# Query and key columns by dimension then head, replicas by three transfers a set

## The chip, the cores and the metric

One core of one Trainium2 chip. The time is the device time of one execution in microseconds (us); a kernel's time is the median of its runs.

## The reference

A cross-attention layer on normalised `x` (8 batches of 512 rows, 256 wide), then a feed-forward layer that is the sum of a dense path (self-attention with 16 heads of 16, and a SiLU network) and a mixture of experts. The change touches the queries and keys of the dense path:

```python
q = (x @ wq).reshape(b, s, H, hd)            # H = 16 heads, hd = 16, s = 512
k = (x @ wk).reshape(b, s, H, hd)
scores = jnp.einsum('bqhd,bkhd->bhqk', q, k) / np.sqrt(hd).astype(np.float32)
scores = jnp.where(causal, scores, jnp.finfo(scores.dtype).min)
attn = jax.nn.softmax(scores, axis=-1)
```

## The kernel before

A program walks the eight batches. Each engine has one instruction queue, taken in order, and all queues follow one list written out by hand, `STEPS`: while batch `b` has its cross-attention, projections and row maxima, batch `c = b - 1` has its attention scores, its SiLU network and its end. Waits are on counting semaphores (`need(engine, batch, name, count)`), `done` counts one up. The first batch has no `c`; in its walk 16 steps `kv` (keys and values of the cross-attention for all batches, stored by ACT's queue to `kt_d` and `vt_d`) take the place of the other work.

Queries and keys are float32 and are multiplied in bf16 as sums of three parts (`part1`, `part2`, `part3`). A score is the sum of six products of parts: q1k1, q1k2, q2k1, q2k2, q1k3, q3k1. To have the six in one product of contraction 96, q and k are replicated: `q_rep` and `k_rep` have 96 rows, one for each of 6 products and each of 16 dimensions, with 16 heads x 512 positions of bf16 = 16,384 bytes in each row. A row is put together through HBM:

- step `qk a` (a = 0, 1 queries, 2, 3 keys; 128 columns each): PE multiplies, ACT makes part 1 (L1178) and part 2 (L1181, L1184), DVE the rest (L1460), POOL part 3 (L720). Each part is a tile of 128 partitions (8 heads x 16 dimensions, head first) x 512 positions.
- SP's queue stores each of the 12 parts to `parts_d` (L524), 128 rows of 1,024 bytes. `parts_d` is (part, q or k, dimension, head, half, position).
- when the six query stores have landed (`q_out`) ACT's queue issues six transfers to `q_rep` (L1202), in the step `route 0`, ahead of the exponential of the router (L1204). When the six key stores have landed (`k_out`) SP's queue issues six to `k_rep` (L531). Each brings 16 rows of 16,384 bytes, one for each dimension. Behind them in SP's queue stand the loads for the next batch (`load_kv`, L451; `load_x`, L444).
- PE goes on with steps `fu` and `fd` (L1033, L1043) of batch `c`, and ranks the router's choice. Then the first step `max` waits for `slot`, `rep_q` and `rep_k` (L942 to L944) before its products (L955, L956), whose maxima DVE takes (L1519). All the 32 `max` steps of a batch and the rest of `fu` and `fd` stand behind it in PE's queue.

The weights `wq` and `wk` are loaded once, with their columns as in the input (head, then dimension). `yb` is a buffer of 1,024 floats a partition that is not used before the end of the first batch.

Of the kernel before, what the change touches and what calls it, by code (L numbers as in the profile page):

```python
# [17 lines left out]
P = 128  # L18
B, S, D = 8, 512, 256
T = S // P  # L20
KD = D // P
CH, CHD, CK = 16, 64, 64
PAIRS = CH // 2
H, HD = 16, 16
NREP = 6
KREP = NREP * HD
# [13 lines left out]
PBUF = 4  # L40
EW_EARLY = 6

Q_PART = (0, 0, 1, 1, 0, 2)
K_PART = (0, 1, 0, 1, 2, 0)

UNITS = 10
CHUNKS = 3
# [6 lines left out]
    sc_ps=4, sc_add=4, sc_sub=4, sc_exp=4, sc_rec=4, sc_nrm=4,  # L54
    pT_ps=8, pT_sb=8, pv_ps=4, xb=1, x1=4, mv2=4, rstd2=4, xn2=4, xT2=2, xn2T=2,
    qk_ps=4, part1=4, rest1=4, part2=4, part3=4, v_ps=4, v_sb=4, lg=4,
    q_out=96, k_out=96, rep_q=96, rep_k=96, z=1,
    gmax=1, gexp=1, mask=1, rank_ps=1, slot=1, xk=1, scat=128, dve_step=42, pool_a=4, pool_n=1,
    a_ps=32, a_max=32, m_part=2, mT_ps=2, mT_sb=2, m_row0=48, m_row1=48,
    b_ps=G * UNITS, b_exp=G * UNITS, b_cut=G * UNITS, va_ps=G * CHUNKS, av_sb=4, avT_ps=4, o_rec=4, o_nrm=4,  # L60
# [139 lines left out]
def xattn_ffn(nc, A, out):  # L200
    per = PER
    counted = {}
    with ExitStack() as ctx:
        def sb(name, shape, dt=F32):
            return ctx.enter_context(nc.sbuf_tensor(name, shape, dt))

        def sem(name):
            return ctx.enter_context(nc.semaphore(name))
# [2 lines left out]

        sems = {n: sem(n) for n in per}
        kv_out = [sem(f"p0_kv_out{i}") for i in range(4)]
        p0 = {n: sem("p0_" + n) for n in ("w_first", "bias_ps", "w_early", "w_mid", "w_late", "w_up", "kv0_ps", "norms", "split_hi", "split", "ident", "const", "iota", "tr_ps", "tr_sb", "kv_ps", "kv_sb", "bk")}

        moe = {n: sem("moe_" + n) for n in ("table_step", "table", "ids_off", "ids", "ew_in", "zero", "gate", "xT_ps", "xT", "up_ps", "th", "u", "g", "gT_ps", "gT", "dn_ps", "eo")}
        xs_in = [sem(f"xs_in{i}") for i in range(4)]
# [6 lines left out]
        wq = sb("wq", [P, KD, D])  # L224
        wk = sb("wk", [P, KD, D])
# [6 lines left out]
        bk = sb("bk", [P, PAIRS])  # L232
# [5 lines left out]
        ident = sb("ident", [P, P])  # L238
# [25 lines left out]
        def part(a, n):  # L264
# [14 lines left out]
        q_rep = part(20480, 4096).bitcast(BF16).rearrange("p (h n) -> p h n", h=H)  # L279
        k_rep = part(24576, 4096).bitcast(BF16).rearrange("p (h n) -> p h n", h=H)  # L280
# [30 lines left out]
        xk_id = part(11264, T * XW).rearrange("p (t w) -> p t w", t=T)  # L311
        yb = sb("yb", [P, T, D])
        hb = sb("hb", [P, T, D])
        xnT = sb("xnT", [P, KD, S])
        xn2T = sb("xn2T", [P, KD, S])
        o_tok = sb("o_tok", [P, T, D])
# [2 lines left out]
        parts = [xnT[:, :, :].rearrange("p k n -> p (k n)").bitcast(BF16).rearrange("p (a n) -> p a n", a=4),  # L319
                 part(13312, 1024).bitcast(BF16).rearrange("p (a n) -> p a n", a=4),  # L320
                 part(14336, 1024).bitcast(BF16).rearrange("p (a n) -> p a n", a=4)]
# [63 lines left out]
        parts_d = internal("parts_d", (3, 2, HD, H // KD, KD, S), BF16)  # L385
# [4 lines left out]
        def done(ins, name, n=1):  # L390

            counted[name] = counted.get(name, 0) + n
            return ins.then_inc(sems[name], n)

        def need(eng, b, name, k):

            eng.wait_ge(sems[name], b * per[name] + k + AHEAD.get(name, 0))
# [42 lines left out]
        def _(sp):  # L440
# [28 lines left out]
            load_x(0)  # L469

            def load_late_weights():
                for dst, src in ((wq, "L0_ffn_wq"), (wk, "L0_ffn_wk")):
                    sp.dma_start(dst[:, :, :], A[src].rearrange("(k p) n -> p k n", p=P)).then_inc(p0["w_late"], 16)
                sp.dma_start(wv[:, :, 0:D], A["L0_ffn_wv"].rearrange("(k p) n -> p k n", p=P)).then_inc(p0["w_late"], 16)
                sp.dma_start(wv[:, :, D:D + E], A["L0_ffn_router_w"].rearrange("(k p) n -> p k n", p=P)).then_inc(p0["w_late"], 16)
                for dst, src in ((wo, "L0_ffn_wo"), (w2, "L0_ffn_w2")):
                    sp.dma_start(dst[:, :, :], A[src].rearrange("(k p) n -> p k n", p=P)).then_inc(p0["w_late"], 16)
                for dst, src in ((aw_bc, "L0_ffn_attn_norm_w"), (fw_bc, "L0_ffn_ff_norm_w"), (mw_bc, "L0_ffn_moe_norm_w")):
                    sp.dma_start(dst[:, :], A[src].partition_broadcast(P)).then_inc(p0["w_late"], 16)
# [35 lines left out]
            def batch(b, c, end=False, only=None):  # L515
                if c is not None:
                    send_shifts(c, 1)
                if b is not None:
                    if c is None:
                        load_late_weights()  # L520
                    for a in range(4):
                        for i, name in enumerate(("part1", "part2", "part3")):
                            need(sp, b, name, a + 1)
                            done(sp.dma_start(parts_d[i, a // 2, :, :, a % 2, :].rearrange("d h n -> h d n"), parts[i][:, a, :]), ("q_out", "k_out")[a // 2], 16)  # L524
                    if c is not None:
                        need(sp, c, "b_ps", per["b_ps"])
                        sp.sem_inc(freed, 1)
                    need(sp, b, "k_out", per["k_out"])
                    for j in range(NREP):
                        src = parts_d[K_PART[j], 1, :, :, :, :].rearrange("d h a n -> d (h a n)")  # L530
                        done(sp.dma_start(k_rep[j:KREP:NREP, :, :].rearrange("d h n -> d (h n)"), src), "rep_k", 16)  # L531
                    if not (isinstance(b, int) and b == B - 1):
                        if c is not None:
                            load_kv(b + 1)
                        load_x(b + 1)
                    send_shifts(b, 0)
                    if c is None:
                        for i in range(4):
                            sp.wait_ge(kv_out[i], 16 * 2 * PAIRS // 4)
                        sp.sem_inc(freed, 1)  # L540
                        load_kv(b + 1)
                    if c is None:
                        need(sp, b, "q_out", per["q_out"])
                        need(sp, b, "pv_ps", per["pv_ps"])
                        need(sp, b, "scat", per["scat"])
                        sp.sem_inc(freed, 1)
                        for dst, src in zip(w13_in, ("L0_ffn_w1", "L0_ffn_w3")):
                            sp.dma_start(dst, A[src].rearrange("(k p) n -> p k n", p=P)).then_inc(p0["w_up"], 16)
                    if b == B - 1:
                        need(sp, b, "pv_ps", per["pv_ps"])  # L550
                        need(sp, b, "q_out", per["q_out"])
                        sp.sem_inc(freed, 1)
                        need(sp, b, "scat", per["scat"])
                        load_experts(range(EW_EARLY))
                if b is None:
                    experts_first()
                elif c is not None:
                    need(sp, c, "y", 1)
                    done(sp.dma_start(at_batch(y_d, c), hb[:, :, :]), "y_out", 16)
# [231 lines left out]
        def _(pe):  # L791
# [31 lines left out]
            def batch(b, c, end=False, only=None):  # L823
# [10 lines left out]
                for step in only or walked(b, c, end):  # L834
                    kind = step[0]
                    if kind == "kv":
                        i = step[1]
# [4 lines left out]
                        w = (wk_c, wv_c)[i % 2]  # L842
# [5 lines left out]
                    elif kind == "m":  # L848

                        i = step[1]  # L850
                        k, half = i // 2, i % 2
# [8 lines left out]
                    elif kind == "bqk":  # L860

                        i = step[1]
# [6 lines left out]
                    elif kind == "vw":  # L869

                        i = step[1]
# [7 lines left out]
                    elif kind == "cs":  # L879
                        t, half = step[1:]  # L880
# [10 lines left out]
                    elif kind == "ct":  # L891
                        t, half = step[1:]
# [9 lines left out]
                    elif kind == "cv":  # L902
                        t, half = step[1:]
# [8 lines left out]
                    elif kind == "qk":  # L912

                        a = step[1]
                        if a == 0:
                            if c is None:
                                pe.wait_ge(p0["w_late"], 16 * 9)
                            need(pe, b, "xn2T", 2)
                        w = (wq, wk)[a // 2]
                        for k in range(KD):  # L920
# [2 lines left out]
                    elif kind == "v":  # L923

                        t = step[1]
# [11 lines left out]
                    elif kind == "max":  # L937

                        hp, t = step[1:]
# [11 lines left out]
                        n = (t + 1) * P  # L951
# [161 lines left out]
        def _(act):  # L1113
# [9 lines left out]
            def batch(b, c, end=False, only=None):  # L1123
# [6 lines left out]
                for step in only or walked(b, c, end):  # L1130
# [63 lines left out]
                            need(act, c, "va_ps", per["va_ps"])  # L1194
                        done(fn(v_heads[:, t, :, 0:HD], bank(t, D).rearrange("p (h d) -> p h d", h=H), ACT.Copy), "v_sb")
                    elif kind == "route" and step[1] == 0:
                        if c is not None:
                            need(act, c, "b_ps", per["b_ps"])
                        need(act, b, "q_out", per["q_out"])
                        for j in range(NREP):  # L1200
                            src = parts_d[Q_PART[j], 0, :, :, :, :].rearrange("d h a n -> d (h a n)")
                            done(act.dma_start(q_rep[j:KREP:NREP, :, :].rearrange("d h n -> d (h n)"), src), "rep_q", 16)  # L1202
                        need(act, b, "gmax", 1)
                        done(fn(g_b, g_a, ACT.Exp), "gexp")  # L1204
                    elif kind == "sc":
# [91 lines left out]
        def _(dve):  # L1297
# [72 lines left out]
            def batch(b, c, end=False, only=None):  # L1370
# [21 lines left out]
                for step in only or walked(b, c, end):  # L1392
# [56 lines left out]
                    elif kind == "qk":  # L1449
                        a = step[1]  # L1450
                        if a == 0 and c is None:

                            dve.wait_ge(p0["w_late"], 16 * 9)
                            for w in (aw_bc, fw_bc, mw_bc):
                                v.tensor_scalar(w[:, :], w[:, :], float(D) ** 0.5, None, ALU.mult).then_inc(p0["norms"], 1)
                            dve.wait_ge(p0["norms"], 3)
# [201 lines left out]
```

## Time and profile before

| | us |
|---|---|
| median of 3 runs (lowest, highest) | 1511.2 (1509.92, 1518.62) |
| profiled execution, its own time | 1514.02 |
| its span on the core | 1512.2 |
| PE busy | 1376.5 (91%) |
| DVE, POOL, ACT busy | 811.6, 601.4, 575.4 |
| mean granted clock of TensorE | 0.962 of full speed |

A busy PE is not a PE at its peak. "SPq" and "ACTq" are the queues of SP and ACT that issue DMAs; the time of such a row is that of the issue, not of the transfer. The DMA share in a window is the mean busy share of the core's 16 DMA engines; it can read above 1 where packets wait on each other. "L955" is line 955 of the kernel.

### The profile page before, as it was taken

How to read it: one execution, taken by the hardware profiler on the slowest of the kernel's cores; microseconds unless marked ns; L12 is line 12 of the kernel's file. 1: busy time of each engine (PE TensorE's matmuls, PEld its weight loads, DVE VectorE, ACT ScalarE, POOL GpSimd, SP SyncE). 2: the span in 40 equal slices, each digit the busy share in tenths (PEclk: the TensorE clock that was granted, in tenths of full speed). 3: DMA queues.
4: the chain of work that ended last, by engine and by line, in shares of the span. 5: the costliest groups of instructions: out<-in, count | busy, mean ns of one | idle time of the engine just before them, and what ended most of it. 6: DMA issues, size and time to landing. Idle time of an engine off the chain costs nothing.

```text
span 1512.2 us, 22383 instructions
## 1 busy us (share of the span) xinstructions
PE 1376.5 (91%) x7229; PEld 891.4 (59%) x7230; DVE 811.6 (54%) x1652; ACT 575.4 (38%) x1214; POOL 601.4 (40%) x1051
## 2 busy tenths in 40 slices
PE   6886898999899989998999899989998789999995
PEld 6543556656665666566656665666566246666673
DVE  2625655754485358436753675366546623333348
ACT  2231553055306521641255036404540444344346
POOL 4312343253325332633254235423532435555544
PEclk8998899999999999999999999999999799999997
DMA  6054205200600060006001500240031424332245
GB/s 209 1 145 138 67 1 130 53 16 1 157 26 16 1 164 19 16 10 170 18 1 39 144 16 1 78 104 16 1 105 50 152 86 129 127 100 87 86 177 197
DMA packets 77529, 115.39 MB, mean 76 GB/s; under 512 B 24072, under 2 KB 65440, under 8 KB 74880
## 3 DMA queue, kind: packets, MB, share of 16 engines
q1 hardware_dynamic: 67120, 79.68, 18.7%
q10 hardware_dynamic: 3840, 16.78, 3.9%
q0 software_dynamic: 6480, 17.77, 3.3%
q8 instruction: 52, 0.85, 0.2%
q14 instruction: 37, 0.30, 0.1%
HBM read 70.22 MB, written 43.59 MB: 75 GB/s over the span
## 4 chain that ended last, share of the span: by engine, by line
PE 66%; DVE 9%; DMA 7%; POOL 5%; ACT 5%; issue 3%; SPq 3%; ACTq 0%; POOLq 0%; DVEq 0%
PE ps L1069 8%; PE ps L1033 8%; PE ps L907 7%; PE ps L888 6%; DVE nm L1519 5%; PE ps L993 5%; PE ps L955 4%; PE ps L1086 4%; PE ps L980 4%; DMA room<-parts_d 3%; PE ps L1043 3%; DMA parts_d<-room 3%; PE ps L921 2%; PE ps L1013 2%; SPq L531 2%
## 5 line engine op out<-in xcount | busy, mean ns | idle before, releaser
L1519 DVE TENSOR_REDUCE nm<-ps 128x2 f32<-128x256 f32 (+3 forms) x256 | 202.4, 819 | 103.3 <-PE ps L956 100.9
L1211 ACT ACTIVATE room<-ps 128x512 f32<-128x512 f32 x320 | 179.7, 598 | 157.0 <-PE ps L980 156.8
L1033 PE MATMUL ps<-hT,w 128*128 128x512 f32 x768 | 212.7, 421 | 0.0
L692 POOL TENSOR_SCALAR_AFFINE_SELECT room<-room 128x256 f32<-128x256 f32 (+1 forms) x320 | 121.5, 391 | 138.3 <-ACT room L1211 133.6
L955 PE MATMUL ps<-room 96*128 96x128 bf16 (+3 forms) x512 | 129.6, 315 | 44.2 <-DMA room<-parts_d 26.5
L1033 PEld LDWEIGHTS ps<-hT,w 128*128 128x128 f32 x768 | 144.7, 196 | 33.1 <-DVE hT L1547 2.0
L1235 ACT ACTIVATE room<-ps 128x512 f32<-128x512 f32 x64 | 37.2, 593 | 294.2 <-PE ps L1033 294.2
L1043 PE MATMUL ps<-w,room 128*128 128x256 f32 x512 | 137.6, 399 | 7.5 <-DVE room L1568 7.5
L1069 PE MATMUL ps<-room 128*128 x284 | 135.4, 599 | 2.4 <-ACT room L1263 2.4
L907 PE MATMUL ps<-room 128*128 128x256 f32 x512 | 123.1, 384 | 2.7 <-ACT room L1172 1.8
L888 PE MATMUL ps<-room,xnT 128*128 128x512 f32 x256 | 122.0, 601 | 0.0
L980 PE MATMUL ps<-room 99*128 99x384 bf16 (+3 forms) x512 | 111.7, 308 | 7.9 <-ACT room L1211 6.0
L955 PEld LDWEIGHTS ps<-room 96*128 96x128 bf16 x512 | 51.6, 102 | 107.7 <-issue 46.9
L907 PEld LDWEIGHTS ps<-room 128*128 128x128 f32 x512 | 93.8, 190 | 22.7 <-issue 6.7
L956 PE MATMUL ps<-mask_qk,ident_b 128*128 128x128 bf16 x512 | 106.1, 228 | 0.0
L1043 PEld LDWEIGHTS ps<-w,room 128*128 128x128 f32 x512 | 91.7, 195 | 24.1 <-DVE room L1568 11.6
L1611 DVE COPY room<-ps 128x256 f32<-128x256 f32 x71 | 30.1, 424 | 125.9 <-PE ps L1077 125.9
L993 PE MATMUL ps<-room,v_aug 128*32 128x512 f32 (+3 forms) x1024 | 91.0, 451 | 6.1 <-POOL room L692 5.1
L1423 DVE TENSOR_TENSOR room<-ps,room 128x1024 f32<-128x1024 f32 x32 | 39.1, 1223 | 106.4 <-PE ps L888 106.4
L980 PEld LDWEIGHTS ps<-room 99*128 99x128 bf16 x512 | 42.8, 98 | 88.7 <-issue 43.7
L641 POOL TENSOR_TENSOR spare_p<-neg_half 128x1 f32<-128x1 f32 x95 | 18.4, 193 | 179.3 <-DVE room L1512 114.7
L781 POOL DMA_INDIRECT pair_d<-room,ids_u x71 | 71.8, 1012 | 33.6 <-issue 29.9
(234 smaller groups left out, 2372.3 us busy)
## 6 DMA issues: line engine op xcount, KB each, us to landing
room<-parts_d SPq DMA_DIRECT2D x48, 256.0 KB, 5.3
room<-parts_d ACTq DMA_DIRECT2D x48, 256.0 KB, 5.7
room<-xs_d SPq DMA_DIRECT2D x71, 129.0 KB, 2.1
parts_d<-room SPq DMA_DIRECT2D x64, 128.0 KB
room<-pair_d SPq DMA_DIRECT2D x8, 1024.0 KB, 8.3
room<-in_L_ffn_ew SPq DMA_DIRECT2D x24, 256.0 KB, 5.5
xin<-in_x SPq DMA_DIRECT2D x8, 512.0 KB, 8.1
parts_d<-xnT SPq DMA_DIRECT2D x32, 128.0 KB
```

Source lines behind the costliest of these rows:

```text
L692: done(g.affine_select(out=w, in_=w, compare_op=ALU.is_ge, fill=0.0, base=0, pattern=[[0, 2]] * (blocks - 1) + [[1, P]], channel_multiplie ...
L888: last = mm(bank(half), xnT[:, k, t * P:(t + 1) * P], m_sb[:, k, half * 512:(half + 1) * 512], start=(k == 0), stop=(k == KD - 1))
L907: last = mm(bank(3, D), pT[:, t % 2, a * P:(a + 1) * P], vw[:, a, :], start=(a == 0), stop=(a == PAIRS - 1))
L955: mm(bank(o, n), q_rep[0:KREP, rep_at(h), t * P:n], k_rep[0:KREP, rep_at(h), 0:n], start=True, stop=False)
L956: last = mm(bank(o, P, t * P), ident_b[:, :], mask_qk[:, :], start=False, stop=True)
L980: last = mm(ps[:, o:o + S - kb * P], k_rep[0:KREP + MROWS, h, kb * P:(kb + 1) * P], q_rep[0:KREP + MROWS, h, kb * P:S], start=True, stop=T ...
L993: last = mm(ps[32 * j:32 * j + 32, 4 * 512 + kb * P:5 * 512], v_aug[:, v_at(kb, 4 * grp + j):v_at(kb, 4 * grp + j) + 32], prob[:, at:at + ...
L1033: last = mm(bank(up_banks(b, m)[i]), w[:, x, k, m * P:(m + 1) * P], hT[:, y, k, :], start=((x, y, k) == terms[0]), stop=((x, y, k) == term ...
L1043: last = mm(bank((6, 7)[half], D, t % 2 * D), gT[:, m % 2, t * P:(t + 1) * P], w2[:, m, :], start=(m == 0 and t % 2 == 0), stop=(m == FB - ...
L1069: last = mm(bank(2 + i % 2), xsT[:, i % 2, k * P:(k + 1) * P], ew[:, bass.ds(at + k * 2 * D, 2 * D)], start=(k == 0), stop=(k == KD - 1))
L1211: done(fn(prob[:, u * 512:(u + 1) * 512], bank(6 + n % 2), ACT.Exp), "b_exp")
L1519: done(v.tensor_reduce(nm[:, t, 2 * hp:2 * hp + 2], pair_ps, AX.X, ALU.max, negate=True), "a_max")
```

## The change

The columns of `wq` and `wk` are brought into the order dimension, then head: they are loaded into `w_heads` (a view of `yb`) and DVE copies them over in the new order, once, ahead of the first `qk` step, which waits for it (`w_turned`). So the partitions of a part are 16 dimensions x 8 heads, and its store to `parts_d` is written as one run over 128 rows where it was 8 heads of 16 rows; the bytes of a row stay 1,024.

The 96 rows of `q_rep` and `k_rep` are ordered by product, then dimension, where it was dimension, then product. Each is filled by three transfers in place of six, of 3, 2 and 1 times 16 rows of 16,384 bytes: for q part 1 three times, part 2 twice, part 3 once (the source has a leading dimension of step 0); for k parts 1 to 3, 1 and 2, 1 (the source's leading dimension is the part). The six products are the same. The three for q go from ACT's queue to SP's, after the stores and ahead of k's.

```diff
-Q_PART = (0, 0, 1, 1, 0, 2)
-K_PART = (0, 1, 0, 1, 2, 0)
+REPLICAS = ((0, 3), (3, 2), (5, 1))
...
+        w_heads = yb[:, :, :].rearrange("p t d -> p (t d)").rearrange("p (i k n) -> p i k n", i=2, k=KD)
...
             def load_late_weights():
-                for dst, src in ((wq, "L0_ffn_wq"), (wk, "L0_ffn_wk")):
-                    sp.dma_start(dst[:, :, :], A[src].rearrange("(k p) n -> p k n", p=P)).then_inc(p0["w_late"], 16)
+                for dst, src in ((w_heads[:, 0, :, :], "L0_ffn_wq"), (w_heads[:, 1, :, :], "L0_ffn_wk")):
+                    sp.dma_start(dst, A[src].rearrange("(k p) n -> p k n", p=P)).then_inc(p0["w_late"], 16)
...
                             need(sp, b, name, a + 1)
-                            done(sp.dma_start(parts_d[i, a // 2, :, :, a % 2, :].rearrange("d h n -> h d n"), parts[i][:, a, :]), ("q_out", "k_out")[a // 2], 16)
+                            done(sp.dma_start(parts_d[i, a // 2, :, :, a % 2, :].rearrange("d h n -> (d h) n"), parts[i][:, a, :]), ("q_out", "k_out")[a // 2], 16)
...
+                    need(sp, b, "q_out", per["q_out"])
+                    for i, (j, n) in enumerate(REPLICAS):
+                        done(sp.dma_start(q_rep[j * HD:(j + n) * HD, :, :].rearrange("p h n -> p (h n)"), parts_d[i, 0, :, :, :, :].rearrange("d h a n -> d (h a n)").unsqueeze(0).to_broadcast([n, HD, H * S])), "rep_q", 16)
                     need(sp, b, "k_out", per["k_out"])
-                    for j in range(NREP):
-                        src = parts_d[K_PART[j], 1, :, :, :, :].rearrange("d h a n -> d (h a n)")
-                        done(sp.dma_start(k_rep[j:KREP:NREP, :, :].rearrange("d h n -> d (h n)"), src), "rep_k", 16)
+                    for i, (j, n) in enumerate(REPLICAS):
+                        done(sp.dma_start(k_rep[j * HD:(j + n) * HD, :, :].rearrange("p h n -> p (h n)"), parts_d[0:n, 1, :, :, :, :].rearrange("i d h a n -> i d (h a n)")), "rep_k", 16)
...
                                 pe.wait_ge(p0["w_late"], 16 * 9)
+                                pe.wait_ge(p0["w_turned"], 2)
...
                     elif kind == "route" and step[1] == 0:
-                        if c is not None:
-                            need(act, c, "b_ps", per["b_ps"])
-                        need(act, b, "q_out", per["q_out"])
-                        for j in range(NREP):
-                            src = parts_d[Q_PART[j], 0, :, :, :, :].rearrange("d h a n -> d (h a n)")
-                            done(act.dma_start(q_rep[j:KREP:NREP, :, :].rearrange("d h n -> d (h n)"), src), "rep_q", 16)
                         need(act, b, "gmax", 1)
...
                             dve.wait_ge(p0["w_late"], 16 * 9)
+                            for i, w in enumerate((wq, wk)):
+                                v.tensor_copy(w[:, :, :].rearrange("p k (a d h) -> p (k a) d h", a=KD, d=HD),
+                                              w_heads[:, i, :, :].rearrange("p k (a h d) -> p (k a) d h", a=KD, d=HD)).then_inc(p0["w_turned"], 1)
```

## Rows read from the trace of the kernel before

**Rows 1.** The page: span, and the chain that ended last by engine and line.
```profile
span 1512.2 us, 22383 instructions
...
PE ps L1069 8%; PE ps L1033 8%; PE ps L907 7%; PE ps L888 6%; DVE nm L1519 5%; PE ps L993 5%; PE ps L955 4%; PE ps L1086 4%; PE ps L980 4%; DMA room<-parts_d 3%; PE ps L1043 3%; DMA parts_d<-room 3%; PE ps L921 2%; PE ps L1013 2%; SPq L531 2%
```

**Rows 2.** Waits of the whole run, PE's: total, times, longest (us).
```profile
PE ps L955 <- DMA room<-parts_d: 26.5, 7, 4.3
```

**Rows 3.** The chain of waits, 388 to 416 us: start, us, what.
```profile
393.43 6.76 DMA parts_d<-room
...
403.36 0.59 SPq L531
...
403.99 7.03 DMA room<-parts_d
411.02 0.25 issue
411.27 0.27 PE ps L955
```

**Rows 4.** Timeline, 376 to 416 us: start, us, engine, line, instruction.
```profile
382.84 0.60 SPq L524 DMA_DIRECT2D parts_d<-xnT  x1
...
390.41 2.28 POOL L720 TENSOR_TENSOR room<-xin,room 128x512 bf16<-128x512 f32 x2
...
392.82 1.18 SPq L524 DMA_DIRECT2D parts_d<-room  x2
...
393.25 3.73 ACTq L1202 DMA_DIRECT2D room<-parts_d  x6
...
397.02 0.23 ACT L1204 ACTIVATE small<-small 128x32 f32<-128x32 f32 x1 [3.45 <-issue]
...
407.71 0.17 DVE L1512 COPY room<-ids_all 128x4 uint32<-128x4 uint32 x1
```

**Rows 5.** DMA from 382 to 391 us: busy tenths in 40 slices, packets.
```profile
DMA  0000000003445300000444522445554555545555
...
DMA packets 862, 0.83 MB, mean 93 GB/s; under 512 B 48, under 2 KB 862, under 8 KB 862
```

**Rows 6.** DMA from 388 to 394 us, 40 slices: busy tenths, GB/s.
```profile
DMA  4545544555454555555455555542000053435564
GB/s 171 205 171 178 171 177 177 191 178 198 177 205 171 171 171 164 191 184 157 157 198 184 191 184 198 184 171 96 27 0 0 0 102 55 75 130 205 178 191 157
```

**Rows 7.** Windows: us, busy time by engine, granted clock, DMA share of 16 engines, GB/s.
```profile
156.00:158.00 2.00, 0.88 (x5) 0.39 (x4) 2.00 (x5) 0.00 (x0) 0.00 (x0) 0.50 1.03 414
391.50:392.00 0.50, 0.50 (x4) 0.43 (x3) 0.50 (x1) 0.43 (x1) 0.50 (x2) 1.00 0.54 191
394.50:395.00 0.50, 0.50 (x3) 0.39 (x3) 0.50 (x1) 0.00 (x0) 0.50 (x1) 1.00 1.35 449
396.00:400.00 4.00, 3.44 (x16) 2.52 (x15) 2.05 (x7) 1.21 (x3) 0.00 (x0) 1.00 1.06 273
408.00:411.00 3.00, 0.00 (x0) 0.00 (x0) 0.00 (x0) 0.00 (x0) 0.15 (x1) 0.75 1.10 119
411.00:416.00 5.00, 4.73 (x17) 3.55 (x18) 1.79 (x4) 0.00 (x0) 1.08 (x1) 0.50 0.80 171
```

**Rows 8.** Timeline of the first batch, 76 to 126 us.
```profile
79.48 0.28 DVE L1455 TENSOR_SCALAR aw_bc<-aw_bc 128x256 f32<-128x256 f32 x1
...
81.05 5.37 PE L921 MATMUL ps<-xn2T,wq 128*128 128x512 f32 x8 [0.78 <-ACT xn2T L1128]
...
93.72 1.36 SPq L524 DMA_DIRECT2D parts_d<-room  x2
...
122.82 0.22 PE L955 MATMUL ps<-room 96*128 96x128 bf16 x1
```

**Rows 9.** Timeline: the first product for the maxima of the eighth batch.
```profile
1140.04 0.27 PE L955 MATMUL ps<-room 96*128 96x128 bf16 x1 [3.37 <-DMA room<-parts_d]
```

More of the change, by code:

```diff
@@ L56 @@
     qk_ps=4, part1=4, rest1=4, part2=4, part3=4, v_ps=4, v_sb=4, lg=4,
-    q_out=96, k_out=96, rep_q=96, rep_k=96, z=1,
+    q_out=96, k_out=96, rep_q=48, rep_k=48, z=1,
     gmax=1, gexp=1, mask=1, rank_ps=1, slot=1, xk=1, scat=128, dve_step=42, pool_a=4, pool_n=1,
@@ L213, in xattn_ffn @@
         kv_out = [sem(f"p0_kv_out{i}") for i in range(4)]
-        p0 = {n: sem("p0_" + n) for n in ("w_first", "bias_ps", "w_early", "w_mid", "w_late", "w_up", "kv0_ps", "norms", "split_hi", "split", "ident", "const", "iota", "tr_ps", "tr_sb", "kv_ps", "kv_sb", "bk")}
+        p0 = {n: sem("p0_" + n) for n in ("w_first", "bias_ps", "w_early", "w_mid", "w_late", "w_turned", "w_up", "kv0_ps", "norms", "split_hi", "split", "ident", "const", "iota", "tr_ps", "tr_sb", "kv_ps", "kv_sb", "bk")}
         moe = {n: sem("moe_" + n) for n in ("table_step", "table", "ids_off", "ids", "ew_in", "zero", "gate", "xT_ps", "xT", "up_ps", "th", "u", "g", "gT_ps", "gT", "dn_ps", "eo")}
```

## The prediction

> **What bounds the kernel now.** I read first the page [rows 1]: PE carries most of the chain that ended last, but two DMA entries stand in it with 3% each, `parts_d<-room` and `room<-parts_d`, and the queue's L531 with 2%. The transfers that the change touches are on the path. Then the list of waits [rows 2]: PE stands before L955 for the replicas in 7 of the 8 batches, 26.5 us in all, 4.3 at most. Then the chain of one batch, the third, in order of time [rows 3]: the stores of the last key part take 6.76 us to land from 393.43, six issues of k's replicas run to 403.95, the last takes 7.03 us to 411.02, and PE starts at 411.27. In the window before that PE has nothing to do (0.00 busy from 408 to 411 [rows 7]), and the other thing that the first maximum waits for, `slot`, is ready at 407.9 [rows 4]. So whatever makes the replicas later than 408 costs its full length, in each batch; what makes them earlier gives at most some 3 us.
>
> Next, how the transfers use the 16 DMA engines, since the change writes all of them anew. From 388 to 392 us only stores are under way; several are queued, and SP is held up in issuing them. The share of DMA time stays at four or five tenths, with 160 to 200 GB/s, in slice after slice [rows 6], 0.54 at 391.5 [rows 7]. As soon as q's replicas come in beside them it is 1.35 with 449 GB/s [rows 7]. So the limit before was not memory: half the engines were at work. The packets say which half rule: 48 of under 512 bytes from 382 to 391 [rows 5]; the remaining 814 are 1 KB rows of some 6.4 stores, so each completed store of 128 rows closes with 8 small packets. Eight is the outermost dimension of the store's target in L524 (8 heads of 16 rows); its other side has 128 partitions. What the trace shows, then: a transfer is spread over as many engines as its outermost dimension allows, and the smaller side decides. And since stores queued one behind another never fill more than half, they all take the same engines, not the next free ones.
>
> The Trainium skill, "DMA: Bandwidth & Descriptors", section "Rules for kernel authors", states the same: an outermost dimension of size c under 16, "a leading zero-stride broadcast of c copies" for instance, confines a DMA to at most c engines, and its section on the semaphore's 16 says that these are the lowest-numbered ones. The rows above agree with both; the rule speaks for the new stores and against the new replicas.
>
> **The change part by part.**
>
> *Stores.* Target and source now both have 128 rows outermost: 16 engines. The backlog goes; the last part is ready when POOL ends at 392.69 [rows 4], and its store is issued by 393.3 in place of 394.0.
>
> *q's replicas* go to SP. The queue passes `b_ps` and `q_out` (q's stores have long landed: ACT got past the same wait at 393.25 [rows 4]) and issues at 393.3. A transfer starts 1.2 us after its issue begins (382.84 [rows 4], first busy slice at 384.0 [rows 5]), so 394.5. The source has outermost 3, 2 and (a leading 1 doesn't count) 16. So the first runs on 3 engines with 16 rows each, the second on 2 with 16 rows each, the third on 16 with one. On the same lowest engines this adds up: the first engine carries 16 + 16 + 1 = 33 rows of 16,384 bytes, the second too. Before, six transfers gave each engine 6 rows.
>
> *One engine's rate.* The best window is 414 GB/s at a share of 1.03 [rows 7]: 25.9 GB/s an engine. The stores on eight engines give 184 / 8 = 23.0 [rows 6]. With all 16 busy on mixed rows it is 273 / 16 = 17.1 [rows 7], but there memory is shared by all. With two or three engines at work nothing else limits one, so I take 25.9: 0.633 us a row, 20.9 us for 33 rows.
>
> The Trainium skill's figure (the same page, "Specifications"), about 27 GiB/s an engine, is 29 GB/s and would make it 18.6 us; no row here shows it.
>
> *k's replicas* wait for `k_out`. The last store took 6.76 us [rows 3] on half the engines beside q's replicas; whether it now takes half or the same, and though three issues for six save some 2 us of L531, k is issued by 402 at the latest, and the same two engines have q's rows in their queue until 394.5 + 20.9 = 415.4. So nothing is bought there. k's 33 rows follow: 394.5 + 2 x 20.9 = 436.3, with 0.3 for the last landing and 0.25 to PE's start [rows 3] 436.9. It was 411.27: **+25.6 us**. The other engines lie idle meanwhile.
>
> *What hides it.* Nothing: PE takes its queue in order, and behind L955 stand the 32 maxima and the rest of the SiLU network. It runs dry before 408, as it did [rows 7]. Batches 2 to 8 repeat this pattern (seven waits [rows 2]; the eighth batch: 3.37 us of it, then the first product at 1140.04 [rows 9]): 7 x 25.6 = 179.
>
> *ACT* loses six issues, 3.73 us [rows 4], ahead of the router's exponential, which waited 3.45 for them. The routing chain gets earlier by that, and stands ready while PE waits for replicas: 0. If the replicas were not late, this would be a part of the gain.
>
> *The queue behind.* The next batch's loads (L451, L444) are queued on the two slow engines behind the replicas and land as much later. They are used from some 40 us after the first maximum on, which itself is as late: 0.
>
> *First batch.* The last store's issue ends at 95.1 [rows 8]; q starts at 96.3. In this walk ACT's queue stores keys and values of 256 KB (eleven `kv` steps ahead of the first maximum, of which some nine fall in this time). They go over 16 engines, 16 KB on each, and take turns with the rows on the slow ones: 9 x 0.633 = 5.7. End: 96.3 + 41.8 + 5.7 + 0.5 = 144.3 against 122.82 [rows 8]: +21.5.
>
> *Weights.* Two DVE copies of 128 x 512 once. L1455's 256 columns take 0.28 [rows 8], so 0.56 each, up to twice that with the stride: 1.1 to 2.2 us. DVE comes to this place at 79.5, PE starts at 81.05 when ACT has turned its operand [rows 8]: 0 to 1, I take 0.5. If that cover were gone it would be 2 us, once.
>
> *Clock.* After the stall now, PE runs at half clock from 411 to 416 [rows 7]. After a stall seven times as long the same stretch returns; I allow 0.5 us more a batch, 4 in all (0 to 20).
>
> Sum: 179 + 21.5 + 0.5 + 4 = 205. Against the profiled execution's 1514.0 that is 1719; the median lies 2.8 lower, so **1716**.
>
> Bounds of this case: at 23.0 GB/s an engine 33 rows take 23.5 us, +5.2 a batch, 42 in all; at 17.1, +21 a batch, far above. A little under 25.9's time is possible too (slices at 205 GB/s over eight engines [rows 6] are 25.6, not more, but slices are coarse), and if k's or q's rows overlap better with the wait, 3 to 5 us a batch less. Own range 1660 to 1800.
>
> **The rivals.**
>
> *A, spread as intended.* Building the instruction, the software could split the leading 3 and 2 so that all 16 engines serve (nothing in the old kernel shows a source of that form; the stores show that it did not do so for an 8). Then the last key store lands in about half of its 6.76 us, at 396.7 in place of 400.2, k's issues take 1.8 in place of 3.8 [rows 3], and 3 MB of replicas at the 273 GB/s of [rows 7] need 11.5 us from 394.5: 406, plus landing. `slot` comes some us earlier with ACT's issues gone, PE is done shortly before 408. The first maximum is then at about 408 in place of 411.3: 3.3 x 7 = 23, and some 3 in the first batch. 1511 - 26 = **1485**. This is the other side. It decides at the point where a transfer's rows on the busiest engine are 6 a set, not 33: the break-even lies near (411.3 - 394.5) / 0.633 / 2 = 13 rows a set. Against it: the flat half share of the stores.
>
> *B, confined but not stacked.* Each transfer takes other engines, or only one of the two sets is confined. Then the busiest engine has 16 to 17 rows a set, 21.5 us for both (or 20.9 for one): 394.5 + 21.5 = 416 to 419 with the later issue of k, +6.5 a batch: **1565**. Against it: queued stores never filled more than eight engines [rows 6].
>
> *C, the stall costs less than its length* because half of it hides under other work. Nothing but PE's own order could do it, and 0.00 of PE, ACT and DVE from 408 to 411 [rows 7] speaks against it; I give it no chance of its own.
>
> **How the numbers follow.** Stacked on few engines 0.85, A 0.10, B 0.05. The forecast is that of the first. Its own range of 1660 to 1800 holds it 0.93 times; that is 0.79 of all, so I widen the low end a little, to 1650, for cases between it and B: 0.8. A measurement of this kernel can tell about 1% from no change. A gives faster by over 1% in 0.07 and within 1% in 0.03; everything else is slower: 0.90.
>
> **What would show each step.** Right: stores alone push the DMA share well above 0.55, with 16 small packets each; between the last store and the first maximum the share falls to 2 or 3 of 16 (0.12 to 0.19) with 50 to 80 GB/s; PE's wait at L955 for `room<-parts_d` is near 30 us in each of seven batches, some 205 in all; time to landing of the replicas is 20 to 40 us. ACT's L1204 no longer waits for issues. Wrong: a share near 1 in that stretch (A); a wait near 10 us (B); a rate per engine far from 26 GB/s moves the result in proportion (1 GB/s is some 13 us).

## The result, and the profile after

The changed kernel takes 1802.4 us (median of 4, 1800.28 to 1804.55); its ratio to the kernel before is 1.191, 95% interval 1.187 to 1.195. It is 19% slower, where 1716 (+13.5%) was forecast and the range ended at 1800.

The page of the changed kernel (the second row is the busy time by engine, the third the granted clock by slice, then the queue of SP, the chain by engine, and the group of the products for the maxima):

```profile
span 1802.8 us, 22330 instructions
...
PE 1383.1 (77%) x7229; PEld 896.6 (50%) x7230; DVE 813.8 (45%) x1654; ACT 576.4 (32%) x1214; POOL 602.6 (33%) x1051
...
PEclk8977897799879986998699969995999588999998
...
q1 hardware_dynamic: 68224, 92.27, 16.7%
...
PE 61%; another core or an unknown queue 16%; DVE 8%; POOL 4%; ACT 4%; DMA 4%; issue 2%; SPq 0%; POOLq 0%; ACTq 0%; DVEq 0%
...
L958 PE MATMUL ps<-room 96*128 96x128 bf16 (+3 forms) x512 | 130.0, 316 | 325.6 <-DMA room<-parts_d 308.0
```

PE's work is nearly the same, 1383.1 us for 1376.5, in a span that is 290.6 us longer. The chain has a new entry of 16% that the profile can't name; the group L958 (L955 before) tells what it is: idle before it for 325.6 us, 308.0 of them for `room<-parts_d`. In the waits the same stands with count and longest:

```profile
PE ps L958 <- DMA room<-parts_d: 308.0, 8, 42.4
```

Eight waits of up to 42.4 us stand where there were seven of up to 4.3 [rows 2]. 308.0 - 26.5 = 281.5 of the 290.6 us. The clock row has 5, 6 and 7 in the slices of the stalls: while PE stands idle the granted clock falls, to 0.50 (1.2 GHz) in the second window below.

SP's queue in the third batch, the issues of the last stores, of q's and k's replicas and of the next batch's loads:

```profile
461.13 0.94 SPq L524 DMA_DIRECT2D parts_d<-room  x2
462.21 1.92 SPq L530 DMA_DIRECT2D room<-parts_d  x3
464.18 1.85 SPq L533 DMA_DIRECT2D room<-parts_d  x3
466.07 27.27 SPq L451 DMA_DIRECT2D room<-kt_d  x2
493.38 19.94 SPq L451 DMA_DIRECT2D room<-vt_d  x2
```

And what the others do meanwhile:

```profile
463.82 0.23 ACT L1201 ACTIVATE small<-small 128x32 f32<-128x32 f32 x1 [1.55 <-DVE small L1470]
...
475.33 0.17 DVE L1512 COPY room<-ids_all 128x4 uint32<-128x4 uint32 x1
...
517.27 0.26 PE L958 MATMUL ps<-room 96*128 96x128 bf16 x1 [42.09 <-DMA room<-parts_d]
```

The exponential of the router (L1201) waits for no issue any more and `slot` is ready at 475.3, all long before PE starts at 517.27. From q's first issue to PE's first product it is 55.1 us; before it was 18.0 [rows 3, 4]. The number is used below for every kernel, "the replica time" of the third batch. The other batches from the second on lie within 2.3 us of it in every kernel, so differences of 1 or 2 us in it tell little.

Two windows inside the stall (the last two columns are the share of 16 engines and GB/s):

```profile
476.00:484.00 8.00, 0.00 (x0) 0.00 (x0) 0.00 (x0) 0.00 (x0) 0.00 (x0) 0.64 0.20 55
498.00:502.00 4.00, 0.00 (x0) 0.00 (x0) 0.00 (x0) 0.00 (x0) 0.00 (x0) 0.50 0.12 49
```

0.20 x 16 = 3.2 engines at first, 0.12 x 16 = 1.9 later: as the transfers' leading 3 and 2. The packets say it exactly. If a store closes with 16 small packets for 8, and the six transfers of a set with 3, 2 and 16, the queue of SP has 96 x 8 = 768 more for the stores, and for replicas 16 sets x (96 rows + 21) = 1872 where it had 48 x 32 = 1536: 67,120 + 768 + 336 = 68,224, the number on the page.

In the second window two engines move 49 GB/s, 24.5 each; in so short a window one row more or less shows. In the first, three engines move 55: 18.3 each, 0.9 us a row as a mean. There is the surprise. The trace also keeps a start and a length for every packet, and a row is one packet of 16,384 bytes. Nearly all of those from 486 to 513 us take 0.61 or 0.62 us (26.7 GB/s). From 476 to 484 us one engine takes 0.61 as well, and the two others start their rows together, within 0.1 us, and mostly take 1.22 to 1.30: the 1.2 us that the expectations below speak of. The packets don't name their engine, but chained end to start they fall into streams, and of the 66, 66 and 34 rows that the three have in a batch, 49, 37 and 17 are still to come at 485.5 us. So the two slow ones have done 17 rows each and the fast one 29: slow are the third engine and one of the two with 66 rows. That one is ready at 516.5 us, the other at 508.9.

### The profile page after: what moved, and what is told of

Its sections match the earlier page's. It is cut to its first block, busy times and chain, and to the rows that moved or that the text cites. A ratio compares the mean times of both kernels' runs of the same rounds, so it can differ in the third digit from the quotient of the medians.

```text
span 1802.8 us, 22330 instructions
## 1 busy us (share of the span) xinstructions
PE 1383.1 (77%) x7229; PEld 896.6 (50%) x7230; DVE 813.8 (45%) x1654; ACT 576.4 (32%) x1214; POOL 602.6 (33%) x1051
## 3 DMA queue, kind: packets, MB, share of 16 engines
q1 hardware_dynamic: 68224, 92.27, 16.7%
## 4 chain that ended last, share of the span: by engine, by line
PE 61%; another core or an unknown queue 16%; DVE 8%; POOL 4%; ACT 4%; DMA 4%; issue 2%; SPq 0%; POOLq 0%; ACTq 0%; DVEq 0%
PE ps L1036 11%; PE ps L1072 7%; PE ps L909 6%; PE ps L890 5%; DVE nm L1519 4%; PE ps L996 4%; PE ps L1046 4%; PE ps L958 4%; PE ps L1089 3%; PE ps L983 3%; DMA room<-parts_d 3%; PE ps L1016 2%; PE ps L924 2%; PE ps L860 1%
## 5 line engine op out<-in xcount | busy, mean ns | idle before, releaser
L958 PE MATMUL ps<-room 96*128 96x128 bf16 (+3 forms) x512 | 130.0, 316 | 325.6 <-DMA room<-parts_d 308.0
L958 PEld LDWEIGHTS ps<-room 96*128 96x128 bf16 x512 | 51.6, 102 | 390.3 <-issue 330.0
L738 POOL DMA_INDIRECT xs_d<-xn_id,idx_u x32 | 31.9, 996 | 331.7 <-DVE nm L1519 286.8
```

What stands on the lines that cost most here:

```text
L958: mm(bank(o, n), q_rep[0:KREP, rep_at(h), t * P:n], k_rep[0:KREP, rep_at(h), 0:n], start=True, stop=False)
```

## The experiments

Each was run beside the kernel before. Times are medians; the kernel before drifted between 1512 and 1519 us from one group of runs to the next, so ratios are compared.

| kernel | us | ratio (95%) | replica time, us |
|---|---|---|---|
| before | 1512.4 | 1 | 18.0 |
| changed | 1802.4 | 1.191 (1.187 to 1.195) | 55.1 |
| e1 q from distinct parts | 1796.7 | 1.184 (1.180 to 1.188) | 53.5 |
| e2 k from one part | 1807.2 | 1.191 (1.187 to 1.196) | 54.7 |
| e3 six transfers, SP | 1597.5 | 1.053 (1.050 to 1.056) | 28.3 |
| e4 six transfers, q on ACT | 1598.7 | 1.053 (1.050 to 1.056) | 28.2 |
| e5 as e4, rows 6 apart | 1491.8 | 0.984 (0.981 to 0.987) | 15.6 |
| e6 as e3, rows 6 apart | 1501.0 | 0.989 (0.986 to 0.993) | 16.7 |
| e7 as e4, rows 2 apart | 1506.4 | 0.993 (0.991 to 0.995) | 17.3 |
| e8 pairs | 1787.9 | 1.178 (1.173 to 1.184) | 51.9 |
| e9 pairs, rows spread | 1752.7 | 1.156 (1.150 to 1.161) | 47.5 |
| e10 pairs, rows 32 apart in step | 1797.3 | 1.185 (1.178 to 1.192) | 53.0 |
| e11 three wide, SP | 1501.9 | 0.990 (0.987 to 0.993) | 16.1 |
| e12 three wide, q on ACT | 1498.4 | 0.988 (0.985 to 0.990) | 16.7 |

**What makes the first rows slow? (e1, e2)** The first idea was the source: three engines copy the same 16 rows of part 1 at the same moment, and k's, which read distinct parts, seemed to go faster.

```diff
 e1: -parts_d[i, 0, ...].unsqueeze(0).to_broadcast([n, HD, H * S])
     +parts_d[0:n, 0, ...].rearrange("i d h a n -> i d (h a n)")
 e2: the reverse for k
```

> The changed kernel, but q's transfers of 3 and 2 copies read parts 1 to 3 and 1 to 2 in place of one part several times (as k's do); destinations, row counts and engines are the same, the products that are summed are not. Theory (engines that copy the same rows at the same moment slow one another to 1.2 us a row of 16 KB): q's rows go at 0.61 us like k's, the wait before the first maximum falls by some 11 us in each of batches 2 to 8, and the time is 1710 to 1725 us. Rival (the slow rows come from the neighbouring destination rows, or from starting beside the stores): no change, 1802 us.

> The changed kernel, but k's transfers of 3 and 2 also read one part several times, as q's do (other products). Theory of the same source: k's rows slow down to 1.2 us as well, some 8 to 12 us more in each batch, 1870 to 1900 us. Rival: no change, 1802 us.

1796.7 and 1807.2 us: neither moved as the theory said, and in e1 two engines still take 1.2 us a row where the third takes 0.61. Reading the same source several times costs 1 us a batch at most (e1 is 6 to 10 us faster in all, where 77 to 92 were expected), and the theory fell.

**Undo the three transfers (e3, e4).** The rest of the change stays; in e4 q's go back to ACT's queue too.

```diff
-for i, (j, n) in enumerate(REPLICAS): ... q_rep[j * HD:(j + n) * HD, :, :], n copies
+for j in range(NREP):
+    src = parts_d[Q_PART[j], 0, :, :, :, :].rearrange("d h a n -> d (h a n)")
+    sp.dma_start(q_rep[j * HD:(j + 1) * HD, :, :].rearrange("p h n -> p (h n)"), src)
```

> The changed kernel with each set as six transfers of 16 rows in place of three; the new column order, the stores in one run of 128 rows and the place of q's transfers in SP's queue stay. If the few engines are the whole loss, PE's wait at the first maximum is 0 to 4 us as before, and the time is 1485 to 1512 us: about 7 us of issue for twelve transfers one after another stand against stores on 16 engines. Rival (q's place in SP's queue costs by itself): 1520 us or more.

> As the run before it, with q's six transfers back in ACT's queue: of the change only the column order, the copies, the row order and the stores on 16 engines are left. The stores are expected to land 3 us earlier and the first maximum to start 2 to 3.3 us earlier in each batch: 1485 to 1500 us. Rival (the replicas themselves, 3 MB a batch, set the time, whenever the stores land): 1505 to 1512 us.

Both at 1.053. Some 70% of the loss went with the few engines. Neither forecast held, and the rivals were off as well. e3 lies above its rival's 1520, but not for the rival's reason, since e4 shows that q's queue makes no difference here; e4 is far above the 1512 us of its own. Some 80 us remain that no part costed in the prediction has. Windows of e4 between k's issues and PE's first product:

```profile
425.00:433.00 8.00, 4.59 (x22) 3.35 (x20) 4.37 (x20) 1.14 (x2) 0.19 (x1) 1.00 1.04 125
433.00:438.00 5.00, 0.00 (x0) 0.00 (x0) 0.00 (x0) 0.00 (x0) 0.00 (x0) 0.52 1.00 118
```

All 16 engines are busy (1.04, 1.00), and move 118 to 125 GB/s: a row takes 16 x 16,384 / 118,000 = 2.2 us. Before, 16 busy engines moved 273 [rows 7]. What is left of the change is the order of the rows in `q_rep` and `k_rep`, and the stores with the new columns.

**The order of the rows alone (e5, e6, e7).** e5 and e6 differ from e4 and e3 in the destination only, e7 puts the rows 2 apart:

```diff
-q_rep[j * HD:(j + 1) * HD, :, :]            # e3, e4
+q_rep[j:KREP:NREP, :, :]                    # e5, e6
+q_rep[j % 3 * 2 * HD + j // 3:(j % 3 + 1) * 2 * HD:2, :, :]    # e7
```

> As the run with six transfers and q in ACT's queue, but the rows of q_rep and k_rep in the old order (the 16 rows of a transfer lie 6 partitions apart, not side by side). Of the change the new column order, the copies and the stores on 16 engines are left. 
> The same with q's six transfers in SP's queue, ahead of k's. Only the queue differs from the run before it: SP issues 12 transfers of 0.6 us one after another, some 2 to 4 us later for the last, against the router's exponential not waiting. 1485 to 1510 us, within 8 us of the run before it.

> As with six transfers and q in ACT's queue, rows of a transfer 2 partitions apart (32 partitions in all). If what counts is how many groups of four neighbouring partitions the 16 rows fall into (4 when side by side, 8 here, 13 or 14 when 6 apart), a row takes about 1.2 us (two share 0.61 each) and the time is 5 to 25 us above the run with rows 6 apart. Rival (only directly adjacent rows hurt): no difference from rows 6 apart; (any bunching hurts alike): about 1595 us.

e5 takes 1491.8 us, 107 less than e4 for one slice of the destination; it keeps the stores and the new columns, so these are not what slows the replicas. e6 takes 1501.0 us, inside its range, though 9 above e5 where at most 8 were expected; the intervals of the two ratios just overlap. Windows of e5, then of e7:

```profile
388.00:392.00 4.00, 3.46 (x16) 2.60 (x15) 2.68 (x10) 1.21 (x3) 0.00 (x0) 1.00 0.92 221
392.00:398.00 6.00, 6.00 (x30) 4.84 (x29) 5.42 (x21) 0.60 (x1) 0.00 (x0) 1.00 1.07 259
```

```profile
394.00:400.00 6.00, 5.48 (x25) 4.26 (x24) 5.00 (x17) 1.57 (x4) 0.00 (x0) 1.00 1.02 216
```

A row takes 16 x 1.07 x 16,384 / 259,000 = 1.08 us with rows 6 apart, 1.24 with rows 2 apart, 2.2 side by side. In the same order 16 rows fall into 13 or 14, 8 and 4 groups of four neighbouring partitions (with p and p + 32 counted as one). The forecast of 1.2 us for two in a group held, and so did 5 to 25 us above e5 (14.6). The Trainium skill, "SBUF — State Buffer", section "Door 1: the DMA port swizzle", says that DMA bandwidth depends on "how many of the 16 SBUF ports your partitions reach", that four neighbouring partitions share a port, and that + 32 stays on it. Two of the three rates agree: 118 / 4 = 30 and 216 / 8 = 27 GB/s a group, where one engine alone moves 26.7; why 30 is above that no run tells. With 13 or 14 groups it is 19 a group, so there something else limits, which is open too.

**The few engines with better rows (e8, e9, e10).** Each set as two transfers of 2 copies and two of 16 rows: the first two engines carry 34 rows a set (33 before). e8 leaves the rows side by side, e9 puts the pairs on every third row, e10 on every second, so that the two engines write p and p + 32 in step:

```diff
-REPLICAS = ((0, 3), (3, 2), (5, 1))
+Q_SETS = ((0, 2, 0), (2, 2, 1), (4, 1, 0), (5, 1, 2))     # start, copies, part
+K_SETS = ((0, 2, 0), (2, 2, 0), (4, 1, 2), (5, 1, 0))     # first part of two for the pairs
 e9:  starts and steps ((0, 3), (1, 3), (2, 6), (5, 6))
 e10: starts and steps ((0, 2), (1, 2), (64, 2), (65, 2))
```

> The changed kernel with the transfer of three copies cut: each set is two transfers of 2 copies and two of 16 rows, all products right. Two engines carry 34 rows of each set, as against 33 before, and they write to different groups of partitions at the same moment (0 to 15 against 16 to 31). Theory (engines in step that write into the same group halve each other's rate; in the changed kernel the first and the third do): rows at 0.61 us, the first maximum some 26 to 30 us later than in the old kernel, 1715 to 1750 us. Rival (few engines, whatever they write to, go at that rate when q and k follow): 1800 us.

> As the run with pairs, same transfers and engines, but with the destination rows spread: the pairs take every third row (0, 3, ..., 93 and 1, 4, ..., 94), the two transfers of 16 rows every sixth. Theory (the first 8 to 10 us of the run with pairs were slow because 14 engines wrote rows that lie side by side): the two slow engines go at 0.61 us a row from the start, 68 rows of a batch take 42 to 44 us in place of 50, the first maximum starts 45 us after q's first issue in place of 52, and the time is 1715 to 1740 us. Rival (the start is slow because 14 engines beside them read and write at all): 1775 to 1790 us.

> The same transfers, the pairs on every second row (0 to 62, 1 to 63) and the others on 64 to 95: at each moment the two engines write rows p and p + 32. In the changed kernel the rows of the first and the third engine were 32 apart and took 1.2 us, those of the second 0.61. Theory (partitions p and p + 32 share one way in, engines in step halve each other): 64 rows at 1.2 us, some 35 to 40 us more in each batch than with rows every third, 1990 to 2060 us. Rival (32 apart is as good as any other distance): 1715 to 1790 us.

In step, each kernel early in the stretch and late:

e8:

```profile
464.00:470.00 6.00, 6.00 (x29) 4.87 (x28) 4.82 (x16) 0.60 (x1) 0.00 (x0) 1.00 0.85 101
490.00:500.00 10.00, 0.00 (x0) 0.00 (x0) 0.00 (x0) 0.00 (x0) 0.00 (x0) 0.50 0.12 52
```

e9:

```profile
456.00:462.00 6.00, 6.00 (x30) 4.89 (x29) 4.84 (x17) 0.60 (x1) 0.00 (x0) 1.00 0.56 131
480.00:496.00 16.00, 0.00 (x0) 0.00 (x0) 0.00 (x0) 0.00 (x0) 0.00 (x0) 0.50 0.13 53
```

e10:

```profile
464.00:466.00 2.00, 2.00 (x10) 1.41 (x8) 1.24 (x5) 0.60 (x1) 0.00 (x0) 1.00 0.38 82
466.00:468.00 2.00, 2.00 (x12) 1.79 (x12) 1.69 (x8) 0.00 (x0) 0.00 (x0) 1.00 0.13 33
468.00:472.00 4.00, 1.45 (x7) 0.82 (x5) 1.50 (x9) 0.60 (x1) 0.19 (x1) 1.00 0.11 29
472.00:480.00 8.00, 0.00 (x0) 0.00 (x0) 0.00 (x0) 0.00 (x0) 0.00 (x0) 0.60 0.13 47
490.00:500.00 10.00, 0.00 (x0) 0.00 (x0) 0.00 (x0) 0.00 (x0) 0.00 (x0) 0.50 0.12 52
```

e8 missed its 1715 to 1750. In its first 10 us the other 14 engines write rows side by side (101 GB/s at a share of 0.85), and the two that matter are held up as well, with some 2.1 us a row. From 472 us on nearly every row takes 0.61 (two engines together move 52 GB/s late in the stretch), so the loss is at the start. So two engines that write 16 partitions apart do not slow each other, and in the changed kernel the slow engine of the two with 66 rows is the first, 32 partitions from the third. Of the 7.6 us that this had cost there, e8 gives 1.2 back to one more row a set and some 3 to the start: each set now has two transfers of 16 rows side by side where the changed kernel has one. With the rows spread (e9) the start moves 131 GB/s at a share of 0.56, twice as much per busy engine, and 35 us of the time go; 1752.7 is still above the 1715 to 1740 expected. e10 is 45 us above e9, and its second and third row show the sharing itself: two engines (0.13, 0.11 of 16) move 33 and 29 GB/s between them, some 1.0 and 1.1 us a row, where the two of e9 move 53. But from 472 us on it is 47, later 52: the slow part ends early, and the 35 to 40 us a batch of a lasting factor of 2 were missed by far (5.5). The packets show why: the two engines start rows together at 462.5 and drift apart, until by 480 us one is two rows ahead, which is four partitions, and both take 0.61 to 0.62 us a row. In the changed kernel, where the next row is the next partition, the pair stays in step through the first 16 rows.

**The change as it may have been meant (e11, e12).** Three transfers a set, with the 16 dimensions outermost in the source, the copies inside, and the destination on every second row:

```diff
-REPLICAS = ((0, 3), (3, 2), (5, 1))
+REPLICAS = ((0, 3), (1, 2), (65, 1))
-q_rep[j * HD:(j + n) * HD, :, :] <- parts_d[i, 0, ...].unsqueeze(0).to_broadcast([n, HD, H * S])
+q_rep[j:j + 2 * n * HD - 1:2, :, :] <- parts_d[i, 0, ...].unsqueeze(1).to_broadcast([HD, n, H * S])
-parts_d[0:n, 1, ...].rearrange("i d h a n -> i d (h a n)")
+parts_d[0:n, 1, ...].rearrange("i d h a n -> d i (h a n)")
```

> The change with its three transfers a set, but the dimension (16) outermost in the source and the copies inside it, so that 16 engines serve; destination rows every second partition, so that the rows written at one moment are 6, 4 and 2 apart. q in SP's queue. Rows at about 1.07 us, 6 issues in place of 12: as the run with six transfers and q on SP (1501 us) or 2 to 8 us faster, 1490 to 1503 us. Rival (fewer and longer transfers gain nothing since the bytes decide): 1499 to 1503 us.

> The same with q's three transfers in ACT's queue: the best of the parts together. Against six transfers with q on ACT (1492 us) k's last issue ends 2 us earlier and the router waits 2 us less; the wait for replicas there was 16 us in all, so 0 to 12 us are to be had: 1480 to 1492 us.

The same bytes by the same number of transfers as the changed kernel, at 0.990 and 0.988 instead of 1.191. e11 is as fast as e6, inside its range, and inside its rival's too, so it doesn't tell the two apart. e12 missed: 1498.4 us, no faster than e5 though it has half the issues (0.988 against 0.984; the intervals overlap). e5's chain in the third batch, the shortest of its seven:

```profile
384.23 1.83 DMA parts_d<-room
386.08 0.56 SPq L533
...
389.22 10.71 DMA room<-parts_d
399.94 0.25 issue
400.18 0.22 PE ps L958
```

and its queues and `slot`:

```profile
384.54 3.71 ACTq L1205 DMA_DIRECT2D room<-parts_d  x6
...
386.08 3.73 SPq L533 DMA_DIRECT2D room<-parts_d  x6
...
398.99 0.17 DVE L1518 COPY room<-ids_all 128x4 uint32<-128x4 uint32 x1
```

The stores land in 1.83 us (6.76 before [rows 3]), k's replicas are issued at 386.1, and the last lands after 10.71, since 3 MB have to move: PE starts at 400.18, 1.0 us after `slot`. In the other batches it is 1.3 to 3.0 us after `slot`, where it was 2.5 to 3.8 before. Both things that PE waits for are now nearly level, and here the stall is so short that PE's first product runs at full clock (0.22 us, 0.27 before [rows 3]).

e5 has the lowest ratio of all: the changed kernel's stores and weights, the old kernel's replicas.

## Why the prediction was right and wrong

- *What bounds the stretch, and that nothing hides it*: right. 281.5 of 290.6 us are the wait at the first product.
- *A transfer runs on as many engines as its smaller outermost dimension allows, always the same ones*: right, by the count of packets to the last one, by the windows, and by e11, which moves the 16 to the outside (and the rows to every second partition, which by e7 costs 15 us on 16 engines).
- *Stores*: right. They run on 16 engines and land in 1.8 us, and with the old replicas (e5) they give 1.6% (1.3 to 1.9). That is 1487 us on the prediction's scale, near the 1485 of rival A, whose premise was wrong for the change as made; it fits a kernel that keeps six spread transfers.
- *One engine's rate, 25.9 GB/s, 0.633 us a row*: right for an engine left alone, which takes 0.61 to 0.62.
- *"With two or three engines at work nothing else limits one, so I take 25.9: 0.633 us a row, 20.9 us for 33 rows"*: **the step that failed**, for q's first 20.9 us of "394.5 + 2 x 20.9". What limits them is where they write. With q's first issue at 462.2 (forecast 393.3, the rest is what the first two batches lost), PE should have started at 505.8; it was 517.3. The replica time is 55.1 us, not 43.6: 11.5 more. The packets divide it. The first and the second engine have 66 rows each, and the second, which shares with nobody after the start, needs 45.1 us for them where 41.8 was forecast: 3.4 us more. It loses 4.6 in the first 9 us, beside the transfers of 16 rows that lie side by side, and gets 1.3 back since a row takes 0.61 and not 0.633. The first engine needs 7.6 us more than the second for as many rows: it writes in step with the third engine, 32 partitions away. Start and landing have the other 0.5. From 486 us on, all of k's rows on these engines included, nearly every row takes the 0.61 to 0.62 of an engine alone.
- *The size of the miss*: the replica time grew by 36.8 us a batch in the mean of batches 2 to 8 (54.76 against 17.94) where 25.6 was forecast, 78 us in all, and the first batch came 29.3 later (152.14 us against 122.82 [rows 8]) where 21.5 was forecast, 8 more. That is the missing 86. Outside the replica time a batch is 0.5 us longer, which is what was allowed for the clock; no run separates its cause.
- *The order of the rows* is what I put at nothing. I took a row's time from a kernel whose rows lay 6 partitions apart; the section on the change names the new order, the prediction says nothing of what it does. It costs 107 us by itself when 16 engines serve (e4 against e5). On the few engines it makes a smaller part: e9, with 68 rows for 66 and 1.3 us more work, has 47.5 us of replica time, so 55.1 - 46.2 = 8.9 of the 11.5 us go with the placement of the rows. The few engines themselves are the larger loss, and that part was forecast.
- *ACT's issues, the queue behind, the weights*: ACT's issues and the queue were right, at 0; for the weights 0.5 us was allowed, too little to be told: in the nine kernels with the copies and with q in SP's queue, q's first issue of the first batch lies anywhere from 90.9 to 97.8 us. (The six issues of k that the prediction lets end at 403.95 are five; the sixth runs to 404.6. No term of the sum hangs on it.) The two copies take 0.6 us each and end before PE's operand is there:

```profile
83.07 0.61 DVE L1452 COPY wq<-yb 128x512 f32<-128x512 f32 x1
...
83.60 0.60 DVE L1452 COPY wk<-yb 128x512 f32<-128x512 f32 x1
...
84.65 3.67 PE L924 MATMUL ps<-xn2T,wq 128*128 128x512 f32 x8 [0.78 <-ACT xn2T L1131]
```

The loads behind the replicas landed late, as said (`kt_d` after 29.1 us, 6.5 before), and nobody waited:

```profile
parts_d<-room SPq DMA_DIRECT2D x64, 128.0 KB, 1.8
...
room<-kt_d SPq DMA_DIRECT2D x14, 128.0 KB, 29.1
```

## What to carry to other kernels

Before merging transfers into one with a leading dimension of copies or parts, look at the outermost dimension of both sides: outermost sizes of 16 and 128 had all 16 engines here, 8, 3 and 2 had as many engines as that, and transfers so confined took the same ones. Copies belong inside it. Then look at which partitions are written at the same moment: 16 long rows want to lie some 6 partitions apart, not side by side. A row order in on-chip memory that no instruction cares about can still be worth 7% of a kernel, so every change of a destination has to be costed, also where it computes the same.

## What the hardware showed that was not expected

- 16 engines that write 16 KB rows into 16 neighbouring partitions moved 118 GB/s, every second partition 216, every sixth 259; each at a share of 1.0. The share of DMA time can't tell these apart; the GB/s beside it can.
- Two engines that wrote rows 32 partitions apart in step took 1.22 to 1.30 us a row of 16 KB, each of them alone 0.61. Where the rows of each were side by side they stayed in step; with rows 2 apart (e10) they drifted out of it.
- A source read by several engines at once costs 1 us a batch at most (e1, e2: 1.184 and 1.191 against 1.191).
- SP was held for 27.3 us in issuing two loads of 128 KB (L451) while two or three engines had replicas to move and the others were idle (a share of 0.20, then 0.12); before, the same two issues took 1.3 us. That an issue blocks on the fullest of its engines is the likely reason, which no run separates.
- Half the issues (e12 against e5) gave no time back. Why is open: rows 4 and 2 apart in its smaller transfers, by e7, would explain a part.
